# An AdaLN attention block and two local-attention layers on one core: the first group's normalisation, the raising of semaphores, the geometric rows and some loads take other places

## The reference

```
shift, scale, gate (twice) = silu(c) @ wmod                # per batch, 6 x 256 numbers
h   = layernorm(x) * (1 + scale) + shift
xn  = layernorm(h) * ln_g + ln_b
q, k, v = heads(xn @ Wq.T), heads(xn @ Wk.T), heads(xn @ Wv.T)   # 8 heads of 32
q, k = rope(q), rope(k)
attn = softmax(causal(q @ k.T / sqrt(32)));  out = attn @ v
qp, kp = q[..., :3] @ dir, k[..., :3] @ dir                # one number per token and head
geo  = softmax(causal(qp[i] * kp[j]));  geo_out = geo @ v
out  = out + head_scale * (geo_out - out)
x    = x + gate * (h + out @ Wo.T)                         # then two layers of local
                                                           # attention and gated FFN
```

## Time and profile before

| | |
|---|---|
| median of 3 runs | 2799.52 us (2797.24 to 2800.05) |
| the profiled execution | 2807.97 us, its span 2806.3 us |
| PE busy | 2569.5 us (92%) |
| DVE busy | 2177.3 us (78%) |
| ACT busy | 1558.0 us (56%) |
| POOL busy | 544.0 us (19%) |
| mean granted PE clock | 0.954 |

### The profile page before, as it was taken

The page is one execution under the profiler, slowest core; times in us unless marked ns, Lnnn a source line. Parts: engine busy times, 40 slices in busy tenths (PEclk is TensorE's granted clock), DMA queues, the critical chain, the costliest instruction groups (busy, mean ns, idle before and its releaser), DMA issues. The chain is left out here.

```text
span 2806.3 us, 45372 instructions
## 1 busy us (share of the span) xinstructions
PE 2569.5 (92%) x14104; PEld 1551.7 (55%) x14104; DVE 2177.3 (78%) x4594; ACT 1558.0 (56%) x3447; POOL 544.0 (19%) x388
## 2 busy tenths in 40 slices
PE   4995999999999999986999999979979999997998
PEld 1442433333333333324677777668857777775877
DVE  4776999999999999975788888645558888885665
ACT  0221566667666667652566666633436666665442
POOL 0110011111111010105333333200023333331000
PEclk7997899999999999988999999989989999999999
DMA  2334355445454445444100000030020000001121
GB/s 88 114 114 114 87 139 141 116 111 128 113 135 137 121 107 129 115 149 127 66 17 21 16 16 21 16 127 17 12 59 8 9 9 8 9 12 47 45 66 39
DMA packets 124307, 205.19 MB, mean 73 GB/s; under 512 B 22704, under 2 KB 71408, under 8 KB 120800
## 3 DMA queue, kind: packets, MB, share of 16 engines
q1 hardware_dynamic: 109440, 164.23, 21.4%
q0 software_dynamic: 8832, 21.80, 2.7%
q10 hardware_dynamic: 5920, 17.75, 1.7%
HBM read 125.57 MB, written 54.26 MB: 64 GB/s over the span
## 5 line engine op out<-in xcount | busy, mean ns | idle before, releaser
L949 PE MATMUL o_ps<-probs,vx 128*33 128x512 f32 (+3 forms) x2560 | 549.0, 551 | 10.7 <-ACT probs L1004 10.7
L1002 ACT ACTIVATE probs<-st_ps 128x512 f32<-128x512 f32 (+3 forms) x640 | 339.0, 530 | 334.5 <-PE st_ps L934 183.7
L1060 DVE SCALAR_TENSOR_TENSOR geo_x<-geo_rows,kp_t 128x512 f32<-128x512 f32 (+3 forms) x640 | 439.5, 710 | 14.5 <-ACT probs L1004 14.5
L1039 DVE TENSOR_REDUCE chunk_max<-a_ps 128x1 f32<-128x512 f32 (+3 forms) x640 | 359.0, 603 | 42.1 <-PE a_ps L917 36.9
L1004 ACT ACTIVATE probs<-geo_x 128x512 f32<-128x512 f32 (+3 forms) x640 | 360.8, 564 | 12.9 <-DVE geo_x L1066 12.8
L1309 PE MATMUL local_in_ps<-w_local,local_ht 128*128 128x512 f32 x1152 | 324.5, 419 | 9.4 <-ACT local_sq L1451 5.2
L1470 ACT ACTIVATE local_probs<-local_s_ps,local_bias,local_inv 128x256 f32<-128x256 f32 x512 | 282.6, 563 | 13.8 <-DVE local_bias L1565 13.8
L917 PE MATMUL a_ps<-k,q 96*128 96x512 f32 (+3 forms) x640 | 239.7, 449 | 43.6 <-DVE chunk_max L1039 36.2
L1748 PE MATMUL ff_ag_ps<-ff_ht_parts,w 128*128 128x512 f32 (+1 forms) x1056 | 257.8, 402 | 19.5 <-DVE ff_gate L1857 11.3
L949 PEld LDWEIGHTS o_ps<-probs,vx 128*33 128x33 f32 x2560 | 124.4, 112 | 272.7 <-issue 185.1
L1477 ACT ACTIVATE local_pt<-local_pt_ps 128x512 f32<-128x512 f32 x256 | 152.3, 596 | 209.3 <-PE local_pt_ps L1367 201.1
(11 more groups left out here) (175 smaller groups left out, 3833.8 us busy)
## 6 DMA issues: line engine op xcount, KB each, us to landing
geo_rows<-geo SPq DMA_DIRECT2D x64, 512.0 KB, 7.6
q<-q_parts SPq DMA_DIRECT2D x48, 256.0 KB, 4.2
k<-k_parts SPq DMA_DIRECT2D x48, 256.0 KB, 6.4
piece_lo<-in_pieces POOLq DMA_DIRECT2D x15, 768.0 KB, 6.0
weight_parts<-piece_hi SPq DMA_DIRECT2D x15, 768.0 KB, 3.4
weight_parts<-piece_lo SPq DMA_DIRECT2D x15, 768.0 KB, 6.0
raw<-out_t SPq DMA_DIRECT2D x128, 64.0 KB
shares_in<-shares SPq DMA_DIRECT2D x64, 128.0 KB, 4.9
```

The lines of the kernel that those rows point to most:

```text
L949: ins = pe.matmul(o_ps[kind * HALF:kind * HALF + VW, g % 2, off:GTOK], vx[s][:, j, :], probs[:, i % PSLOTS, kind, off:GTOK], start=j == 0, ...
L1002: act.activation(probs[:, s % PSLOTS, 0, off:GTOK], st_ps[:, (b * NB + s) % STBANKS, off:GTOK], ACT.Exp).then_inc(q["st_used"], 1)
L1039: dve.reduce_max(chunk_max[:, it, c:c + 1], a_ps[:, n % ABANKS, 0:width], AX.X).then_inc(q["a_used"], 1)
L1060: ins = dve.scalar_tensor_tensor(out[:, off:GTOK], geo[:, 1, at], kp_t[:, j, ds(b, 1)].rearrange("p o -> p o"), geo[:, 0, at], ALU.add, AL ...
```

## The change

- Setup: SP also loads group 0's `xin`; DVE takes its statistics and normalises it there, while PE makes `mod_ps`. After the matmuls DVE copies only shift and scale, ACT the other four vectors; the gates' magnitudes (`gates`) are made at the end of the first phase.
- SP raises all semaphores in setup (`prime_all`, 138 of them); the two blocks of their own are gone.
- First phase: DVE makes the geometric row of group n - 1 in group n (`directions`), after `modulated` and ahead of the second rotation, with the running values carried in `carry`; the last one follows `gates`. SP stores these rows, `send_geo`, behind the next group's parts. After group 5's parts have landed SP loads the first head's operands.
- Attention phase: no scans; only kp is loaded for PE's transposes, which stand behind the first three maxima. POOL instead of DVE sets the rows of `k3` to 1.
- Last head: SP instead of ACT issues the first local layer's loads, two ahead of `send(b, 0)`, nine behind it and behind the landing of the last weight piece.
- Buffers for this are allocated on the right side or earlier.

```diff
@@ setup_phase
+                sp.dma_start(E.xin[:, :, :], row_tiles(io["x"])[:, 0:GT, :]).then_inc(const_loaded, 16)
...
+                prime_all(sp, S)
+                sp.wait_ge(const_loaded, 32)
...
+                act.wait_ge(stage_done, MOD_DONE)
+                for b in range(B):
+                    act.activation(S.mod[:, 2:6, b, :], mod_ps[:, b, 1:3, :].rearrange("p a (s c) -> p (a s) c", c=C), ACT.Copy)
...
+                dve.wait_ge(const_loaded, 32)
+                c.link(ln_stats(dve, c, E.stats, E.mv, E.carrier[:, :], lambda t: [E.xin[:, t, :]]))
...
+                for b in range(B):
+                    last = dve.tensor_copy(S.mod[:, 0:2, b, :], mod_ps[:, b, 0, :].rearrange("p (s c) -> p s c", c=C))
+                c.link(last)
+                dve.tensor_scalar(S.mod[:, 1, :, :], S.mod[:, 1, :, :], 1.0, None, ALU.add)
@@ qkv_phase
-        prime(nc, q)
...
+                def send_geo(n):
+                    heads, tokens = place(n)
+                    sp.wait_ge(q["geo_ready"], n + 1 + START)
+                    sp.dma_start(S.geo[heads, 1, tokens], run[0][:, :]).then_inc(q["geo_out"], 16)
...
+                sp.wait_ge(q["parts_out"], 16 * 8 * (GROUPS - 2) + START)
+                load_operands(sp, S, 0, S.q3_first, S.k3_first, S.loads[0])
...
+                def directions(n, first):
+
+                    c = Counter(dve, q["scan"], 3, n)
+                    qp, kp = dots_sb[:, 0, :], dots_sb[:, 1, :]
+                    dve.wait_ge(q["dot_used"], 2 * n + 2 + START)
+                    dve.wait_ge(q["geo_out"], 16 * n + START)
+                    dve.tensor_tensor_scan(run[0][:, :], kp, kp, -3.0e38 if first else carry[:, 0:1], ALU.max, ALU.max)
+                    c.link(dve.tensor_tensor_scan(run[1][:, :], kp, kp, 3.0e38 if first else carry[:, 1:2], ALU.min, ALU.min))
+                    for k in range(2):
+                        last = dve.tensor_copy(carry[:, k:k + 1], run[k][:, GTOK - 1:GTOK])
+                    c.link(last)
+                    dve.scalar_tensor_tensor(run[0][:, :], qp, 0.0, run[0][:, :], ALU.is_ge, ALU.mult)
+                    c.link(dve.scalar_tensor_tensor(run[1][:, :], qp, 0.0, run[1][:, :], ALU.is_lt, ALU.mult))
+                    dve.scalar_tensor_tensor(run[0][:, :], run[0][:, :], -1.0, run[1][:, :], ALU.mult, ALU.subtract).then_inc(q["geo_ready"], 1)
...
                             piece(n + 1)
+                        if u == 0 and begun:
+                            directions(n - 1, first)
...
+                gates()
+                directions(GROUPS - 1, False)
@@ attention_phase
+                if not more:
+
+                    sp.wait_ge(q["values_in"], SETS + BH + START)
+                    sp.wait_ge(q["pv_done"], b * NB + PV0 + START)
+                    W.load_inputs(sp, S, 0)
                 send(b, 0, s)
+                if not more:
+                    sp.wait_ge(q["piece_out"], 16 * 2 * (BH - 1) + START)
+                    W.load_tables(sp, S, io, 0)
+                    W.load_output(sp, S, io, 0)
...
-                    if not more and s == 4:
-
-                        act.wait_ge(q["values_in"], BH + START)
-                        act.wait_ge(q["pv_done"], b * NB + PV0 + START)
-                        W.load_local(act, S, io, 0)
```

More of the change, by code:

```diff
@@ L967, in turn @@
                         weigh(b - 1, (s - 1) % SETS, NB - 1)
+            pe.wait_ge(masks_in, 16 * 3)
+            for item in FIRST_ITEMS[:ABANKS]:
+                maxima(*item)
             pe.wait_ge(q["dots_in"], 16 + START)
```

237 lines of the change are left out of this document (135 added, 102 removed).

## The result

The changed kernel took 2774.99 us (median of 4 runs, 2771.26 to 2777.07) against 2799.78 of the kernel before in the same measurement: ratio 0.9911 (95% interval 0.9894 to 0.9928), 24.8 us less. Measured again in five rounds it was 0.9905 (0.9889 to 0.9922), 2774.11 us. The forecast was 2788.0, 11.4 us less, in a range from 2778 to 2801: right in direction, less than half of what came, and 3 us outside the range. The profiled execution of the kernel after took 2774.7 us, its span 2773.0, mean granted clock 0.964; that of the kernel before lay 8 us above its own median, so differences of whole spans between these two traces say too much, and what follows goes by stretches.

What follows compares the result with a forecast made beforehand. Bounds: DVE alone at the start, TensorE and DVE taking turns in the loop, DVE's geometric rows, ACT's DMA issue. Terms -20.1 + 27.9 + 3 - 0.5 - 9.7 - 12 = -11.4 us gave 2788 us, range 2778 to 2801.

Steps and rivals of the forecast that it cites:

- Setup: Setup and first group: statistics and semaphores hidden beside PE's matmuls, first modulation at 23.4 instead of 43.5 us, -20.1 us.
- The loop: Token groups 1 to 6: directions adds 4.65 us each while PE stands still, +27.9 us, plus +3 us for the clock.
- the clock: Loop over token groups: PE's granted clock falls behind each of the six new stalls, +3 us (0 to 10).
- rival A: Loop: the scans hide in DVE's idle 4.11 us a group, no clock loss, 2760 us in all; chance 8%.
- Last group and boundary: End of first phase: late directions, gates and last row against cheaper boundary; attention phase begins at 257.2, -0.5 us.
- The attention phase's start: Scans gone, masks late next: PE may start 9.1 us and DVE 10.1 us into the phase instead of 22.1, -9.7 us.
- The last head: Last head: ACT no longer stands issuing eleven DMAs between two exponentials, SP's issue counted hidden, -12 us (-12.6 to -5).
- Rival B: Last head: SP's issue delays sends or loads, or the head would have stood anyway; 2794 to 2800 us; chance 12%.
- the 1 us that the forecast weighed against its own 12: Last head: by the Trainium skill's rule that issuing engine saves only issue time, the gain would be near 1 us.
- the places are all short stretches, so I carry the microseconds over: Whole kernel: the -11.4 us summed from the profile is applied unchanged to the median 2799.52 us, giving 2788 us.
- C: Loop: the clock stays down between stalls, at 17 us of half speed 40 us in all, 2825 us; chance 8%.
- D: Front: first modulation waits for weights, or maxima for masks as late as before; about 2800 us; chance 5%.

Runs made afterwards that it cites:

- the run with the stall filled: Kernel after, with four matmuls that nothing needs on TensorE in the stall before the fourth projection: 2775.41 us, ratio 0.9911 to the kernel before.
- The early masks: Kernel after, with the masks loaded in the first phase and directions left in place: 2764.83 us, ratio 0.9876 to the kernel before.
- the delay: Kernel before, with 16 linked copies that nothing needs at the end of setup: 2806.58 us, ratio 1.0025.
- the run on the addresses: Kernel after, with an unused buffer of 1 KB a partition in front, moving all later buffers: 2777.69 us, ratio 0.9930 to the kernel before.

## Why the prediction was right or wrong

**Setup: right.** -20.1 forecast, -20.5 seen, and both covers (4.6 us of statistics, 8.8 us of semaphores) showed their full price when taken away.

**The loop: the mechanism was right, the two terms too big by 4 us.** Each step stands in the trace: seven instructions ahead of the second rotation, TensorE waiting for `rot_s`, the clock down in every pass. The price of the seven was right, too: from the first rotation to the second it is 4.60 us in group 0, which is written out and has no `directions`, and 9.12 in group 1, written out with them; in the loop it was 4.97 in the kernel before and is 9.75 after. That makes 4.5 and 4.8 us, and 4.65 was forecast. Two things were left out. The change also takes groups out of the loop: written out, the stretch is 0.37 us shorter by itself, in groups 1, 5 and 6 that is 1.1 us. And the forecast said that the period leaves no slack at the fourth projection, and against rival A that TensorE waits for `rot_s` already. It doesn't: the list above has all waits of its TensorE in these groups, and none is for `rot_s`; instruction by instruction, the fourth projection of the kernel before began 0.23 us behind the end of `rot_s`, the one of the kernel after 0.05 us behind it. That is 0.2 us a group, 1 us in six. By the run with the stall filled the place cost 26.4 us where 27.9 was forecast, and the clock 1.1 (0.9 to 2.9 by the other traces) where 3 was; group 0, whose period got 0.5 us shorter, makes the 26.9 of the table. The Trainium skill, TensorE: Matmul & The Clock Gate, section HAM oscillation, has the clock fall in every pass of such a loop and every fall paid. The traces nearly agree with the first (six falls in six groups in five of seven traces, five in the other two), and only in part with the second: where TensorE waits for another engine later in the pass, that wait takes most of the loss up.

**Last group and boundary: right** (-0.5 forecast, -0.9 seen).

**The attention phase's start: right, 1.5 us short.** The masks were late next, as said; they landed 7.8 us into the phase and not 9.1, and VectorE began 0.8 us behind TensorE and not 1.0.

**The last head: the mechanism was right, 2 us short.** The step that failed is "the stretch took 20.65 us, in the head before 8.02: 12.6 us", taken as what such a stall costs. It is the one trace of three in which the clock came back early; the other two have 22.91 and 23.22, and the mean of the three is 14.2 us over the stretch without loads, near the 14.1 of the last head as a whole. The forecast gave the slow clock behind a stall a term of its own for the stall that the change brings, and didn't look at the clock behind the one that it takes away. Rival B fell: in the kernel after SyncE's longest row of issues is 2.26 us. The term was 14 us, and not near the 1 us that the forecast weighed against its own 12.

**The sum.** All terms erred to the same side: setup by 0.4 us, the loop and its clock by 4.0, the boundary by 0.4, the attention phase's start by 1.5, the last head by about 2. With the terms as seen the gain is 20 us, and the time would be near 2780, inside the range. What took the result out of it is the step "the places are all short stretches, so I carry the microseconds over", which puts everything that the change doesn't touch at nothing: 25 us and more were measured (24.8 and 24.7 by the medians, 24.9 and 26.6 by the ratios, with intervals from 20 to 31), so some 5 to 7 lie there. From the first to the fifteenth load of sums the four kernels with the first phase as before took 842.9, 838.1, 838.3 and 839.1 us (mean 839.6), the thirteen others 832.1 to 841.1 (mean 836.0). Behind the last head it is 1539.5, 1539.2, 1532.2 and 1532.1 against 1528.7 to 1534.9 (mean 1532.0): two of the four show nothing there. In the heads the clock was down for 54 us against 45 on the mean, and over all seventeen traces their time grows by 0.28 us for each us at the low clock (a straight line through them), so that some 2.5 of the 3.6 us go with the clock; why it is low less often is open. The early masks and the delay don't explain it, the run on the addresses gave no clear answer, single traces of one group of kernels lie in the other, and no run was made that tells a lasting effect from chance. The cause of these 5 to 7 us stays open.

**The other rivals.** A (the scans hide) fell with the period of 28.5. It is right about the idle time, not about this place: with the same work ahead of the first rotation 26 of the 27.5 us in the six groups came back. C fell: the clock came back within 7 us of each fall. D fell: the first product stood at 23.08, and the masks released TensorE 7.8 us into the phase.

The range, 2778 to 2801, missed by 3 us. Its lower end is the forecast less all the lower bounds of its terms, 10 us; it had no room for the last head beyond its 12 us, nor for anything outside the terms.

## What to carry to other kernels

Where an engine stands idle, note in which part of the loop: the same 4.6 us, six times over, cost 27.5 us in one place and 1.4 in another, and the other only wanted a second buffer. When a stall goes, count the slow clock behind it as well as the stall, and look at more than one trace, since that part varied from 1 to 3.4 us. A sum over the places that a change touches says nothing of the rest of the kernel: here the rest moved by a fifth of the gain and more.

## What the runs showed of the hardware

- Raising 138 semaphores costs SyncE about 8.8 us, 64 ns each (an estimate from the lengths of the boundaries, borne out by the 7.8 us that came when their cover was taken away), and every other engine too if it stands ahead of a boundary with nothing beside it.
- A copy of 64x8 on VectorE took 1.84 us beside a memset on GpSimd, 0.17 alone.
- TensorE behind a stall of 4.4 us ran eight passes in 6.19 us instead of 3.60, and a whole group lost 0 to 1.1 us by it, since a wait later in the group took the rest up. In the last head, where it stood for some 9 us and ran at half speed for 4.6 to 9.9 us after ScalarE went on, the steps behind the stall took 1.0 to 3.4 us more.
- Eleven loads issued by ScalarE between two exponentials held it for 11.5 us, issued by SyncE they held no engine that another waited for.
